# Full attentions: the value products cut in two halves of 256 queries, with six buffers of exponentials

## The reference, cut to what matters

```python
B, N, C = 2, 1024, 128
def full_attention(x, Wqkv, bqkv, causal):
    q, k, v = split_heads(x @ Wqkv + bqkv)
    s = einsum('bhnd,bhmd->bhnm', q, k) * 8 ** -0.5
    if causal:
        s = where(tril, s, NEG)
    p = softmax(s, axis=-1)
    return merge_heads(einsum('bhnm,bhmd->bhnd', p, v)) @ Wo + bo

x = x + full_attention(layernorm(x), lora)
x = x + channel_mix(layernorm(x))
x = x + full_attention(layernorm(x), causal)
x = x + channel_mix(layernorm(x))
x = x + gated_recurrence(layernorm(x))
x = window_layers(x)
x = x + full_attention(layernorm(x), plain)
x = window_layers(x)
```

## Time and profile before

| what | value |
|---|---|
| median of 3 runs | 6055.75 us (6048.82 to 6063.87) |
| profiled execution | 6068.23 us |
| its span | 6066.2 us |
| TensorE busy | 5514.9 us (91%) |
| VectorE busy | 4303.9 us (71%) |
| ScalarE busy | 4078.8 us (67%) |
| first to last exponential, lora attention | 61.4 to 465.2 us |
| the same, causal attention | 572.1 to 897.4 us |
| the same, plain attention | 3386.9 to 3776.8 us |
| mean granted TensorE clock | 0.953 of 2.4 GHz |

### The profile page before, as it was taken

How to read it: one execution, slowest core, us unless ns; L and a number is a source line. 1 busy time by engine, 2 the same in 40 slices (tenths; PEclk the granted TensorE clock), 3 DMA queues, 4 the chain that set the end, 5 groups by cost and what they waited for, 6 DMA issues and landing times. The chain is left out here.

```text
span 6066.2 us, 154761 instructions
## 1 busy us (share of the span) xinstructions
PE 5514.9 (91%) x57658; PEld 3906.5 (64%) x57658; DVE 4303.9 (71%) x6698; ACT 4078.8 (67%) x7766; POOL 2685.8 (44%) x2411
## 2 busy tenths in 40 slices
PE   8887996799999999999997888799999999999997
PEld 3223332677777777777775323677777777777775
DVE  7875645677777777777774886777767777777774
ACT  5764654577767777777774577677767776776774
POOL 1101100565555555555552110666555555555552
PEclk8987997899999999999998899899999999999998
DMA  0000000100000000000000000100000000000000
GB/s 12 1 1 5 2 1 9 33 18 18 19 16 18 22 17 21 16 19 18 18 21 11 4 1 1 35 17 18 19 15 22 17 17 23 15 18 18 18 21 18
DMA packets 173969, 93.45 MB, mean 15 GB/s; under 512 B 81508, under 2 KB 170112, under 8 KB 173184
## 3 DMA queue, kind: packets, MB, share of 16 engines
q1 hardware_dynamic: 173184, 83.03, 5.1%
HBM read 68.96 MB, written 1.05 MB: 12 GB/s over the span
## 5 line engine op out<-in xcount | busy, mean ns | idle before, releaser
L1745 POOL TENSOR_TENSOR cross<-raw,tab_b 128x512 f32<-128x512 f32 x768 | 990.0, 1314 | 291.9 <-ACT raw L1615 289.1
L732 DVE TENSOR_REDUCE arena<-PS 128x1 f32<-128x512 f32 (+3 forms) x1408 | 838.1, 648 | 251.5 <-PE PS L550 161.3
L683 ACT ACTIVATE arena<-PS 128x1024 f32<-128x1024 f32 (+1 forms) x704 | 656.4, 968 | 328.6 <-PE PS L573 243.1
L1751 POOL CAST kT_b<-kT 128x512 bf16<-128x512 f32 x384 | 273.3, 712 | 1284.5 <-ACT kT L1669 1284.5
L1838 DVE TENSOR_TENSOR oT<-PS,rec_den 128x288 f32<-128x288 f32 (+1 forms) x768 | 327.0, 426 | 642.6 <-ACT rec_den L1649 642.5
L1809 DVE TENSOR_TENSOR rot<-PS,tab_a 128x512 f32<-128x512 f32 x768 | 524.2, 687 | 275.8 <-PE PS L1494 154.5
L1615 ACT COPY raw<-PS 128x512 f32<-128x512 f32 x768 | 448.3, 589 | 328.8 <-PE PS L1494 287.0
L1463 PE MATMUL PS<-qT,kT 64*128 64x96 f32 x8448 | 659.9, 286 | 0.0
L1641 ACT ACTIVATE PT<-PS 128x576 f32<-128x576 f32 (+1 forms) x768 | 468.3, 610 | 255.3 <-PE PS L1463 244.2
L1825 DVE TENSOR_TENSOR rot<-rot,cross 128x1024 f32<-128x1024 f32 x384 | 609.1, 1586 | 11.5 <-POOL cross L1745 11.2
L550 PE MATMUL PS<-k_parts,q_parts 32*128 32x512 f32 (+3 forms) x1408 | 507.2, 510 | 93.0 <-DVE arena L732 78.2
(11 more groups left out here) (253 smaller groups left out, 12942.8 us busy)
## 6 DMA issues: line engine op xcount, KB each, us to landing
w_qk<-in_w_pairs SPq DMA_DIRECT2D x196, 128.0 KB, 2.1
w_v<-in_w_pairs SPq DMA_DIRECT2D x100, 128.0 KB, 2.2
w_o<-in_w_out_pairs SPq DMA_DIRECT2D x192, 64.0 KB, 1.8
xs<-x_tok SPq DMA_DIRECT2D x24, 256.0 KB
xs<-x_tok SPq DMA_DIRECT2D x24, 254.0 KB
w<-in_L_ffn_W SPq DMA_DIRECT2D x12, 341.0 KB
q_parts<-max_rows SPq DMA_DIRECT2D x192, 2.0 KB
raw<-in_c_E SPq DMA_DIRECT2D x2, 896.0 KB, 4.5
```

Of the source, the lines that this page charges most:

```text
L683: nc.scalar.activation(PT[u % 4].rearrange("p (a n) -> p a n", a=2)[:, :, first_q:512], PS[:, 2 * (u % 2):2 * (u % 2) + 2, first_q:512], A ...
L732: nc.vector.tensor_reduce(maxima[:, 2 * m + h, qt, kh:kh + 1], bank[:, 0:keys_of(qt, kh)], AX.X, ALU.max).then_inc(bank_free, 1)
L1745: nc.gpsimd.tensor_tensor(dst[:, :, :, o:o + 32], src[:, :, :, other:other + 32], tab[:, :, o:o + 32].unsqueeze(2).broadcast_to([128, 8, 2 ...
```

## The change

The values of a step are made in two parts of 256 queries: part 0 (queries 0 to 255 of the half) of step t - 1 at the end of slot 1, as before, and part 1 (queries 256 to 511) of step t - 2 at the end of slot 0, one slot later. `pv_done` is counted with part 1. `PT` has six buffers in place of four, and the exponentials wait for the values of step t - 3. In the causal attention each part has one product of zeros ahead of it, and a part whose queries all lie ahead of the keys has nothing else. `out_half`, the fills and their places stay as they are.

```diff
--- before.py
+++ after.py
@@ -371,7 +371,7 @@
             return room.enter_context(nc.sbuf_tensor(f"{name}_{Room.uses}", shape, F32R))
 
         VB = [cut(BT * 128, 0 if m == 0 else None).rearrange("p (t h d) -> p t h d", t=BT, h=4) for m in range(2)]
-        PT = [cut(2 * 512) for m in range(4)]
+        PT = [cut(2 * 512) for m in range(6)]
         OT = [cut(512) for m in range(2)]
         o_tok = cut(HGROUPS * BT * 32).rearrange("p (i t n) -> p i t n", i=HGROUPS, t=BT)
         maxima = cut(64).rearrange("p (h q k) -> p h q k", h=4, q=8)
@@ -585,23 +585,26 @@
                                                     skip_group_check=True)
                         last.then_inc(st_full, 1)
 
-                def values(t):
+                def values(t, part):
                     i, (hf, kt) = t // STEPS, steps[t % STEPS]
-                    first_q = first_query(hf, kt)
-                    pe.wait_ge(exp_done, 2 * t + 2)
-                    if kt == 0:
-                        need(pe, o_ev, 2 * i + hf)
-                    if t % STEPS == 0:
-                        pe.wait_ge(vb_ready, i + 1)
+                    lo, hi = max(first_query(hf, kt), 256 * part), 256 * part + 256
+                    if part == 0:
+                        pe.wait_ge(exp_done, 2 * t + 2)
+                        if kt == 0:
+                            need(pe, o_ev, 2 * i + hf)
+                        if t % STEPS == 0:
+                            pe.wait_ge(vb_ready, i + 1)
                     if causal and kt > 0:
-                        for _ in range(2):
-                            nc.tensor.matmul(PS[:, 6, :].rearrange("p (a n) -> p a n", a=4), nothing, nothing.unsqueeze(1).broadcast_to([128, 4, 128]),
-                                             start=False, stop=False, skip_group_check=True)
-                    for hh in range(4):
-                        last = nc.tensor.matmul(PS[32 * hh:32 * hh + 32, 6, first_q:512], VB[i % 2][:, kt, hh, :],
-                                                PT[(2 * t + hh // 2) % 4][:, 512 * (hh % 2) + first_q:512 * (hh % 2) + 512],
-                                                start=kt == 0, stop=t == last_step(2 * i + hf), tile_position=(0, 32 * hh))
-                    last.then_inc(pv_done, 1)
+                        nc.tensor.matmul(PS[:, 6, :].rearrange("p (a n) -> p a n", a=4), nothing, nothing.unsqueeze(1).broadcast_to([128, 4, 128]),
+                                         start=False, stop=False, skip_group_check=True)
+                    if lo < hi:
+                        for hh in range(4):
+                            last = nc.tensor.matmul(PS[32 * hh:32 * hh + 32, 6, lo:hi], VB[i % 2][:, kt, hh, :],
+                                                    PT[(2 * t + hh // 2) % 6][:, 512 * (hh % 2) + lo:512 * (hh % 2) + hi],
+                                                    start=kt == 0 and part == 0, stop=t == last_step(2 * i + hf), tile_position=(0, 32 * hh),
+                                                    skip_group_check=True)
+                    if part == 1:
+                        last.then_inc(pv_done, 1)
 
                 def fills(t, slot):
                     for name in late(t, slot):
@@ -645,7 +648,9 @@
                             mask_scores(2 * t + slot)
                         fills(t, slot)
                         if slot == 1 and 0 < t <= ALL:
-                            values(t - 1)
+                            values(t - 1, 0)
+                        if slot == 0 and 1 < t <= ALL + 1:
+                            values(t - 2, 1)
 
             @block.scalar
             def _(act):
@@ -678,9 +683,9 @@
                 def exponentials(u):
                     t = u // 2
                     act.wait_ge(st_full, u + 1)
-                    need(act, pv_done, t - 1)
+                    need(act, pv_done, t - 2)
                     first_q = first_query(*steps[t % STEPS])
-                    nc.scalar.activation(PT[u % 4].rearrange("p (a n) -> p a n", a=2)[:, :, first_q:512], PS[:, 2 * (u % 2):2 * (u % 2) + 2, first_q:512],
+                    nc.scalar.activation(PT[u % 6].rearrange("p (a n) -> p a n", a=2)[:, :, first_q:512], PS[:, 2 * (u % 2):2 * (u % 2) + 2, first_q:512],
                                          ACT.Exp).then_inc(exp_done, 1)
 
                 for f in range(4):
```

## The result

The changed kernel takes 6013.8 us (median of 4 runs, 6012.9 to 6021.1), the kernel before 6053.7 (6048.8 to 6063.9) beside it; the ratio is 0.9931, 95% interval 0.9916 to 0.9947. In a second session it was 0.9926 (0.9912 to 0.9941). The forecast of 6036 was 22 us too high; the range held.

A forecast was written before the change was run, and what follows sets the result against it. No engine was full; VectorE's reductions waited while TensorE made 1.00 us of values in a 2.70 us loop. 6068.2 - 35 (lora and plain) - 5 - 15 + 18 + 5 = 6036 us, range 6005 to 6072.

The forecast's parts named there:

- Plain steps: Lora and plain attentions, nine steps a group: 2.40 us for 2.70, set by VectorE's reductions; 2.7 us less a group.
- The tile switch: Between 32-row and 32-column products: a gap only behind the values, none into them; bound 0 to 0.15 us a step.
- Steps with fills: Lora and plain groups: s6 and s14 -0.24 us each, s10 -0.43, s0 and s3 -0.05 each, s2 -0.40.
- The copy of bank 6: In s1, held behind a piece and a half of values, starting at 2.28: step 5.25 us, +1.65; in s9 +0.15.
- Causal groups: Causal attention: TensorE gaps +1.9 us, held copies s1 +0.5 and s5 +0.65, fourth product's wait -3.9; about -0.8 a group.
- The fall in the sixth lora group: 14.8 us for a clock fall to 1.2 GHz, begun in a step with rows, counted as gone: -15 us.
- The clock, +18: Twelve held s1 steps, each 1.8 us without TensorE work, risk a clock fall: 1.5 us each, bounds 0 and 14.8.
- Causal attention, -5 and +5: Causal attention in all: -5 us, between -20 and +15; another +5 for the clock in s5 of its groups.
- The second case of the prediction: Rival: halves fit and the idle of s1 is too short to matter, the clock holds; 6013 us, chance 0.22.
- the rows' DMAs: Rival: the DMAs of the rows become the limit; if all 28 halves lose 0.3 us, 6044 us; chance 0.07.
- the switch's second side: Rival: the switch of tiling costs on both sides; 126 plain steps near 2.55 us, 6055 us, chance 0.16.
- cost nothing: Buffers 5 and 6 of `PT` cost nothing: they let the exponentials wait for values a step older.

The follow-up runs named there:

- the two runs that part them: Changed kernel with part 1 of a half's last values ahead of the fills: 5981.3 us; changed kernel with lora and plain pieces in s0, s3, s4, s5: 5983.6 us.
- the halves together: Changed kernel with both parts of a step's values at the end of slot 1, six buffers kept: 6063.6 us, ratio 1.0003 to the kernel before.
- the repeat: The changed kernel as it is, measured again in the second session: 6014.1 us, ratio 0.9926 to the kernel before.
- the run with fewer zeros: Changed kernel without the product of zeros where a part has no queries: 6016.0 us, ratio 0.9928 to the kernel before.
- the ending half first: Changed kernel with part 1 of a half's last values ahead of the fills of its slot: 5981.3 us, ratio 0.9880 to the kernel before.
- four buffers: Changed kernel with four `PT` buffers in place of six, exponentials waiting for the values of step t - 2: 6195.5 us, ratio 1.0237.

## Why the prediction was right or wrong

Right, by the steps of the prediction:

- *Plain steps* at 2.40: measured 2.39, VectorE without idle time. A half cost 0.56 to 0.57, as taken from the earlier trace rows.
- *The tile switch*: 0.43 into the values and a gap only behind them, as by the row. The changed kernel has twice as many switches, and its plain steps stay at 2.40. The Trainium skill's rule (TensorEngine Tiling (Array Packing), Key Properties: a change of tiling mode drains TensorE) could show on that one side alone here; whether the gap is the drain, no run tells.
- *Steps with fills*: s4 to s15 of a plain group take 30.8 us; the walk had 34.4 - 3.5 = 30.9. s2 took 4.38 for 4.41, s3 3.25 for 3.24, s10 3.09 for 3.09. Wrong was s0, 3.62 for 3.24: the walk let its piece follow the product at once, but it waits for its bank.
- *The copy of bank 6*: held as foreseen. s1 took 5.44 for 5.25; the piece had to wait for the ring, since step s0's reductions were not done, so the copy began at 2.45, not 2.28. Groups took 47.5 where 47.1 was worked out: 0.4 more in s0, 0.2 in s1, 0.1 less in s4 to s15. That the hold is the piece's doing was argued; the two runs that part them show it.
- *Causal groups*: 0.7 less where 0.8 was expected, in part by luck: s1 cost 1.0 in place of 0.5 and s5 0.7 for 0.65, and the other steps gave 2.4 for 2.0.
- *The fall in the sixth lora group* was gone, -15 as counted, but the reason given, denser steps with rows, is not shown, and the number came in part by luck. With the halves together these steps are as they were (3.3 us), and that group had no fall either (49.5 us). The profiled execution lies 12 to 14 us above the medians of the two sets of runs beside it, so its fall need not be there in every execution of the kernel before: against the median the gain is 40 us, not the 55 of the spans.

Off, all in one direction, 6036 less 6013.4 of the profiled execution, 23 us:

- *The clock, +18.* The mechanism was right, the number and the price were not. Seven of twelve held steps brought a fall in place of all twelve; a short one costs 48.7 - 47.5 = 1.2 us, the one of 6.8 us 49.3 - 47.5 = 1.8, in all 6 x 1.2 + 1.8 = 9. I had priced them from the long fall and the causal ones, but pieces follow at once, and the clock was back after 3.4 or 6.8 us.
- *Causal attention, -5 and +5.* Measured -11. The sum carried on the falls of the profiled execution before (groups of 42.8, 43.8 and 43.9 for 40.0, 10.5 us) and added more for the copy in s5. In the changed kernel the falls that begin behind the first step are three of 6.8 us in place of five of 6.8 to 10.2, and of the five full groups behind the first, one shows a fall (41.8, 2.5 us more), in the repeat two (42.2 and 41.7). I should have counted falls as what differs between executions.
- 3.9 us came from stretches without any change. With 9 from the clock and 11 from the causal attention that is 24, less 1 by which the other terms were too favourable. Larger parts cancel behind this 1: the twelve groups fell short by 12 x 0.4 = 5 and the first ones by 2, while the last ones gave 4.8 where 0.8 was put (the terms beside it add up to 0.6), 2 of it because a fall in the last plain group of the kernel before was gone.

The second case of the prediction gave 6013, the measured time, but for a reason that is false: the clock did not hold in s1. It is the forecast's mechanism with smaller prices that the traces show. The rivals of the rows' DMAs and of the switch's second side left next to no trace: plain steps did not stay at 2.55, and in the plain attention the scores waited for these DMAs once, 0.7 us.

The sentence that the buffers "cost nothing" was right and too short: it never worked out what stands behind them, 3% of the time (ratios of 1.0237 and 0.9931).

## What to carry to other kernels

Where one engine makes short work for another and long work for itself in program order, cut the long work and put the pieces between; the cut alone gives nothing. Then walk through every step in which something else waits for the end of the part that moved: here one copy, one slot later and behind a fill, took back 12 x 1.8 us in s1 and 9 us in falls, over half of what the halves had brought in the lora and plain attentions, and keeping fills out of its way gave that back. An average does not show it, since the idle time before the reductions was 14.0 and 13.0 us in two groups while it had moved: from 3.5 us in s0 to s3 and 3.5 in s4 to s15 of each group to 5.8 and 0.7.

## What the runs showed of the hardware

- TensorE's clock fell to 1.2 GHz during or up to 1.0 us behind 1.67 us without work at the end of s1, in seven of twelve groups of one execution, eight of the repeat and seven of the run with fewer zeros; with gaps of 1.01 us, the ending half first, in none of twelve. With pieces (128x128 products) right behind the gap it was back at 2.4 GHz after 3.4 to 6.8 us. In the kernel before one fall lasted 44.4 us, over a stretch whose only products on the full array were the four transposes of s10, and ended with the next pieces; with the halves together one of 13.7 us ended behind 2.1 us of other 128x128 products.
- In the lora and plain attentions of both versions with steps of 2.70 (the kernel before and the halves together) such a fall began in a step with rows; in the eight executions with steps of 2.40 none began there. In seven of these none that began within the two attentions lasted over 6.8 us, but with four buffers one in each last group, which has no pieces, lasted 30.7. This is a count of few, not a measured rule, and shorter steps alone do not keep the clock up.
- Sixteen products of 256 columns in four column tiles took the 1.00 us of eight with 512: where nothing stands between the halves, the cut itself cost nothing.
